# Attention scores over 64 rows in both row halves, from separate q and k

## The chip, the cores and the metric

The kernel runs on one core of one Trainium2 chip. The metric is the device time of one launch in microseconds. Before the change three runs took 1321.24 to 1322.76 us, with a median of 1322.1 us. The profile comes from one more execution.

## The reference

The kernel computes one transformer layer in fp32. There are 16 sequences of 256 tokens with 128 features.

```
x = x + attention(layernorm(x))        # 16 heads of 64
q, k, v = x @ Wq, x @ Wk, x @ Wv       # [16, 256, 16, 64]
w = softmax(q @ k.T / sqrt(64))
attention = (w @ v) @ Wo + bo
x = x + ffn(layernorm(x))              # 160 experts, top 8 of sigmoid scores
routed = sum over the chosen experts of weight * w_down @ silu(w_gate @ x)
shared = w_down_shared @ silu(w_gate_shared @ x)
```

## The kernel before, in words

The program has two stages. The first does attention, routing and the scatter of the normalised tokens into expert blocks of 64 rows in DRAM (`slot_x`). The second loads these blocks, runs the experts over them, stores the results (`block_y`), and gathers and combines them per token. The change touches the first stage alone.

The first stage is a software pipeline that is written out by hand and has the same form on each engine: `body(b)` for sequence b, with a loop over the 8 head pairs g. `step = 8 b + g`. In one body an engine works on several steps at once: on TensorE the scores of step - 1, the first products psY of this step, the values of every second step, the probabilities times values (psO) of step - 3, the transposes of the probabilities (psT) of step - 2, and the output projection (psA) of step - 4. Sequences 0 to 3 and the drain are straight code, 4 to 15 a hardware loop (`sequences`). All instructions of an engine run in the order of the code. Waits are on semaphores, which count how often a producer has finished: `p_ok` counts the exponentials (four a step), `s_ps` the scores of a head (two a step), `yq_ps`, `yh_ok` and `yl_ok` the psY products and their high and low parts, `c_in` and `x_in` the loads of small constants and of the tokens behind the first sequence.

Scores are not formed from q and k. At the start TensorE forms, for each head, m = Wq Wk^T (L529, 64 rows deep, heads alternating), and ScalarE and VectorE split m into a high and a low part (L645, L909). Then y = m^T x for two heads (psY), and the scores are y times the normalised tokens themselves, which ScalarE copies per sequence as `key_hi` and `key_lo` (L659, L660). Each product of split operands takes three matmuls: high by high, high by low, low by high (`split_product`). Matmuls of the scores run over all 128 rows of the array, first all six of head 0, then the six of head 1.

After the scores VectorE takes the negated row maxima (`negmax`, L1085), ScalarE the exponentials (L668), VectorE the reciprocal of the row sums (`rinv`), GpSimd three of the four multiplies by it (L795) and ScalarE the fourth (L682). TensorE transposes the result into psT, ScalarE copies it to `pT_sb` (L278).

From sequence 2 on VectorE also computes the routing of the sequence two before, one piece in each head pair (`choose`, `slots`, ... `blocks`), for which TensorE adds the ranks (L504 to L511, at g = 1), and GpSimd scatters 16 rows of indices by indirect DMA (L820), three or four of them in each of the head pairs 6, 7, 0, 1 and 2.

SyncE issues the loads in the order of the code, then the zero fill of `slot_x` and later parts of the fill and the expert weights, paced by `s_ps`.

Of the kernel before, what the change touches and what calls it, by code (L numbers as in the profile page):

```python
# [23 lines left out]
P = 128  # L24
# [39 lines left out]
def build(nc, x, wqT, wkT, wv, wo, bo, rwT, ebias, wgd, wgsT, wdsT, out):  # L64
# [4 lines left out]
    with ExitStack() as ctx:  # L69
# [36 lines left out]
        with actx:  # L106
# [61 lines left out]
            m_hi = sa("m_hi", [D, H, D], F32R)  # L168
            m_lo = sa("m_lo", [D, H, D], F32R)
# [7 lines left out]
            key_hi = sa("key_hi", [D, SEQ], F32R)  # L177
            key_lo = sa("key_lo", [D, SEQ], F32R)
            y_hi = sa("y_hi", [D, 2, 2, SEQ], F32R)
            y_lo = sa("y_lo", [D, 2, 2, SEQ], F32R)  # L180
# [13 lines left out]
            wqT_sb = sa("wqT_sb", [P, G, D])  # L194
            wkT_sb = sa("wkT_sb", [P, G, D])
# [31 lines left out]
        for name in """x0_in x_in wq_in wk_in wv_in c_in we_in zfill_a zfill_b yfill m_ps w_hi_ok w_lo_ok  # L227
                ln1_st ln1_ag ln1_ve ln1_rs ln1_xn xt_ps xt_hi xt_lo key_ok
# [55 lines left out]
        def _(sp):  # L284
            xv = x.rearrange("b s d -> (b s) d").rearrange("(n p) d -> p n d", p=P)
            sp.dma_start(x_res[:, 0:TB, :], xv[:, 0:TB, :]).then_inc(s["x0_in"], 16)
            sp.dma_start(wqT_sb[:], wqT.rearrange("(g p) d -> p g d", p=P)).then_inc(s["wq_in"], 16)
            sp.dma_start(wkT_sb[:], wkT.rearrange("(g p) d -> p g d", p=P)).then_inc(s["wk_in"], 16)
            sp.dma_start(wv_sb[:], wv).then_inc(s["wv_in"], 16)
            sp.dma_start(x_res[:, TB:NT, :], xv[:, TB:NT, :]).then_inc(s["x_in"], 16)  # L290
# [101 lines left out]
        def _(pe):  # L392
# [6 lines left out]

            def body(b):  # L400
                for g in range(G):
                    step = G * b + g
                    if live(b, g, 1):
                        u = step - 1
                        wait(pe, s["yh_ok"], u + 1)
                        wait(pe, s["yl_ok"], u + 1)
                        wait(pe, s["key_ok"], 2 * b if g == 0 else 2 * b + 2)
                        for h in range(2):
                            wait(pe, s["p_ok"], 4 * u - 2 + 2 * h)
                            for qt in range(TB):  # L410
# [228 lines left out]
        def _(act):  # L639
            act.wait_ge(s["wv_in"], 16)  # L640
            act.copy(wv_hi[:], wv_sb[:]).then_inc(s["w_hi_ok"], 1)
            act.wait_ge(s["m_ps"], 1)
            for k in range(4):

                act.activation(heads(m_hi, k), (psS, psT)[k // 2][:, k % 2, :].rearrange("p (g d) -> p g d", g=4),  # L645
                               ACT.Copy, scale=DH ** -0.5).then_inc(s["w_hi_ok"], 1)

            def body(b):
                for g in range(G):
                    step = G * b + g  # L650
                    if live(b, g, 0):
                        wait(act, s["yq_ps"], step + 1)
                        wait(act, s["s_ps"], 2 * (step - 1))
                        act.copy(y_hi[:, g % 2].rearrange("p a t -> p (a t)"), psY[:, 0, :]).then_inc(s["yh_ok"], 1)  # L654
                    if g == 0 and live(b, g, 0):
                        wait(act, s["s_ps"], 2 * step)
                        wait(act, s["xt_hi"], b + 1)
                        wait(act, s["xt_lo"], b + 1)
                        act.copy(key_hi[:], xnT_hi[:].bitcast(F32)).then_inc(s["key_ok"], 1)  # L659
                        act.copy(key_lo[:], xnT_lo[:].bitcast(F32)).then_inc(s["key_ok"], 1)  # L660
# [206 lines left out]
        def _(dve):  # L867
# [22 lines left out]
            def input_split(b):  # L890
# [14 lines left out]
            dve.wait_ge(s["w_hi_ok"], 1)  # L905
            dve.tensor_tensor(wv_lo[:], wv_sb[:], wv_hi[:].bitcast(F32), ALU.subtract).then_inc(s["w_lo_ok"], 1)
# [345 lines left out]
```

## Time and profile before

| | |
|---|---|
| median of three runs | 1322.1 us |
| the profiled execution | 1333.29 us, span 1331.9 us |
| mean granted TensorE clock | 0.835 |
| busy, TensorE, VectorE, ScalarE, GpSimd | 940.9, 848.5, 684.3, 740.5 us |
| attention with routing | from 22 us to about 735 us |
| q1, all loads and stores | 110.56 MB |

The profiled execution is 11.2 us above the median. Busy time of an engine is the time in which one of its instructions runs; TensorE's matmuls overlap, so its busy time is not its load. "Idle before" an instruction is followed by what released it. In the tables PE is TensorE, PEld its weight loads, DVE VectorE, ACT ScalarE, POOL GpSimd and SP SyncE.

### The profile page before, as it was taken

Reading aid. Unit: us, or ns where it says so; the run is one execution under the profiler, and the core shown is the slowest. Engines: PE = TensorE matmul, PEld = TensorE weight load, DVE = VectorE, ACT = ScalarE, POOL = GpSimd, SP = SyncE. Lnnn points to the kernel's source line nnn. Section 1 sums busy time; section 2 is a strip of 40 time slices with the busy share of each in tenths; the row PEclk is TensorE's granted clock in tenths of the full one; section 3 lists DMA queues with packets and bytes.
Section 4 is the critical chain, followed back from the end, with each engine's and each line's share of the span. In section 5 each row is a group of like instructions: output and inputs, shape, how many; then the busy total and the mean of one; then the engine's idle time right before and its main releaser. Section 6 shows DMA issues by size and latency. Waiting matters only on the chain.

```text
span 1331.9 us, 30438 instructions
## 1 busy us (share of the span) xinstructions
PE 940.9 (71%) x8654; PEld 770.8 (58%) x8654; DVE 848.5 (64%) x2817; ACT 684.3 (51%) x2015; POOL 740.5 (56%) x989
## 2 busy tenths in 40 slices
PE   4999999999999999999999448955566657200000
PEld 3888888878888888888887226633444445100000
DVE  3568889888888888888888635732555445532222
ACT  2878777777777777777778103722333333100000
POOL 1334766776676567666766570044443344677774
PEclk7999999999999999999999656966876677555555
DMA  8402432333233000012220624843544444221211
GB/s 298 190 1 96 155 120 114 120 121 117 112 122 120 18 20 32 24 51 77 91 81 22 259 85 133 266 129 130 156 158 155 141 137 143 87 59 58 57 57 35
DMA packets 64252, 144.65 MB, mean 109 GB/s; under 512 B 12496, under 2 KB 20624, under 8 KB 64208
## 3 DMA queue, kind: packets, MB, share of 16 engines
q1 hardware_dynamic: 47824, 110.56, 23.2%
q0 software_dynamic: 16384, 33.59, 8.3%
q8 instruction: 18, 0.29, 0.1%
q14 instruction: 26, 0.21, 0.1%
HBM read 59.16 MB, written 84.93 MB: 108 GB/s over the span
## 4 chain that ended last, share of the span: by engine, by line
PE 38%; issue 19%; DVE 14%; POOL 12%; ACT 6%; another core or an unknown queue 6%; DVEq 3%; DMA 1%; ACTq 0%; POOLq 0%; SPq 0%
POOL yg L843 10%; PE psS L396 8%; PE psT L449 6%; PE psY L396 5%; PE psO L434 5%; DVE w_b L1182 4%; ACT p_sb L668 3%; PE psS L606 2%; PE psA L459 2%; PE psT L596 2%; DVEq L245 2%; PE psVM L396 1%; POOL slot_x L820 1%; DVE xn L887 1%
## 5 line engine op out<-in xcount | busy, mean ns | idle before, releaser
L843 POOL DMA_INDIRECT yg<-block_y,tok_idx x256 | 247.3, 966 | 253.0 <-DMA block_y<-y_b 110.8
L795 POOL TENSOR_SCALAR p_sb<-p_sb,rinv 128x256 f32<-128x256 f32 x384 | 191.3, 512 | 219.5 <-DVE rinv L1075 215.0
L820 POOL DMA_INDIRECT slot_x<-xn_src,slot_u x256 | 255.7, 999 | 79.7 <-issue 75.4
L668 ACT ACTIVATE p_sb<-psS,negmax 128x256 f32<-128x256 f32 x512 | 236.6, 480 | 31.8 <-DVE negmax L1085 30.7
L1182 DVE COPY w_b<-w_all 128x192 f32 x672 | 129.9, 265 | 156.5 <-remote 106.3
L1085 DVE TENSOR_REDUCE negmax<-psS 128x2 f32<-128x512 f32 x256 | 167.4, 684 | 30.6 <-PE psS L396 14.4
L396 PE MATMUL psS<-key_hi,y_hi 128*128 128x256 f32 x512 | 157.8, 308 | 7.2 <-ACT p_sb L668 5.7
L434 PE MATMUL psO<-pT_sb,v_sb 128*64 128x256 f32 x1024 | 138.8, 391 | 21.6 <-ACT pT_sb L278 21.4
L278 ACT COPY pT_sb<-psT 128x512 f32<-128x512 f32 x256 | 141.7, 617 | 12.4 <-PE psT L449 6.6
L396 PE MATMUL psS<-key_hi,y_lo 128*128 128x256 f32 x512 | 144.7, 283 | 0.0
L396 PE MATMUL psS<-key_lo,y_hi 128*128 128x256 f32 x512 | 144.6, 282 | 0.0
L449 PE MATMUL psT<-ident,p_sb 128*128 128x128 f32 x1024 | 138.1, 278 | 2.1 <-POOL p_sb L795 2.1
L449 PEld LDWEIGHTS psT<-ident,p_sb 128*128 128x128 f32 x1024 | 113.5, 142 | 27.4 <-issue 18.8
L654 ACT CAST y_hi<-psY 128x512 fp32r<-128x512 f32 x128 | 75.1, 587 | 100.8 <-PE psY L396 96.6
L606 PE MATMUL psS<-xbT,w_b 128*64 128x64 f32 x1344 | 82.2, 256 | 60.6 <-issue 56.2
L1189 DVE TENSOR_TENSOR yg<-yg,wE_res 128x1024 f32<-128x1024 f32 x32 | 39.1, 1221 | 119.9 <-DMA yg<-block_y,tok_idx 119.5
L1090 DVE TENSOR_TENSOR y_lo<-psY,y_hi 128x512 fp32r<-128x512 f32 x128 | 87.7, 685 | 41.1 <-ACT y_hi L654 39.0
L606 PEld LDWEIGHTS psS<-xbT,w_b 128*64 128x64 f32 x1344 | 63.7, 162 | 86.0 <-issue 85.3
L668 ACT ACTIVATION_READ_ACCUMULATOR p_sb<-psS,negmax 128x1 f32 x512 | 108.0, 211 | 0.0
L396 PEld LDWEIGHTS psS<-key_hi,y_hi 128*128 128x128 f32 x512 | 97.7, 191 | 11.9 <-ACT p_sb L668 6.4
L396 PEld LDWEIGHTS psS<-key_lo,y_hi 128*128 128x128 f32 x512 | 97.9, 191 | 0.0
L396 PEld LDWEIGHTS psS<-key_hi,y_lo 128*128 128x128 f32 x512 | 97.4, 190 | 0.0
(175 smaller groups left out, 2107.8 us busy)
## 6 DMA issues: line engine op xcount, KB each, us to landing
block_y<-zero SPq DMA_DIRECT2D x21, 1024.0 KB
xb<-slot_x SPq DMA_DIRECT2D x84, 256.0 KB
block_y<-y_b SPq DMA_DIRECT2D x84, 256.0 KB
w_all<-in_wgd_dram SPq DMA_DIRECT2D x16, 960.0 KB
slot_x<-zero SPq DMA_DIRECT2D x1, 11264.0 KB, 34.3
slot_x<-zero SPq DMA_DIRECT2D x10, 1024.0 KB
slot_x<-xn_src,slot_u POOLq DMA_INDIRECT x256
yg<-block_y,tok_idx POOLq DMA_INDIRECT x256
```

Source lines behind the costliest of these rows:

```text
L278: copy(pT_sb[:, (g - 2) % 2, h].rearrange("p a t -> p (a t)"), psT[:, h, :]).then_inc(s[f"pt{h}_ok"], 1)
L396: m = pe.matmul(dst, wsl[a], xsl[c], start=(n == 0), stop=(n == 2))
L434: m = pe.matmul(psO[h * DH:(h + 1) * DH, 0, 0:SEQ], v_sb[:, (g - 3) // 2 % 2, kt, (g - 3) % 2, h * DH:(h + 1) * DH], pT_sb[:, (g - 3) % 2, ...
L449: m = pe.transpose(psT[:, h, kt * SEQ + qt * P:kt * SEQ + (qt + 1) * P], p_sb[:, (g - 2) % 2, h, qt, kt * P:(kt + 1) * P], ident[:])
L606: m = pe.matmul(psS[half, par, cols], w_b[:, r, i, 0:INTER], xbT[:, par, :, i * P // GB:(i + 1) * P // GB], start=True, stop=True)
L668: act.activation(p_sb[:, (g - 1) % 2, h, qt, :], psS[:, h, qt * SEQ:(qt + 1) * SEQ], ACT.Exp, bias=negmax[:, (g - 1) % 2, h, qt:qt + 1], s ...
L795: pool.tensor_scalar(pq, pq, rinv[:, (g - 1) % 2, k // 2, k % 2:k % 2 + 1], 1.0, ALU.mult, ALU.mult).then_inc(s["pn_ok"], 1)
L820: pool.indirect_dma_start(slot_x, bass.IndirectOffsetOnAxis(ap=slot_u[:, i, j:j + 1], axis=0), xn2_src[:, i, :], None).then_inc(s["scat"], 16)
L843: pool.indirect_dma_start(yg[:, r, k, :], None, block_y, bass.IndirectOffsetOnAxis(ap=tok_idx[:, par, r, k:k + 1], axis=0)).then_inc(gat[r ...
L1085: dve.tensor_reduce(negmax[:, (g - 1) % 2, h, :], psS[:, h, :].rearrange("p (i k) -> p i k", i=TB), AX.X, ALU.max, negate=True).then_inc(s ...
L1090: dve.tensor_tensor(y_lo[:, g % 2].rearrange("p a t -> p (a t)"), psY[:, 0, :], y_hi[:, g % 2].rearrange("p a t -> p (a t)").bitcast(F32), ...
L1182: m = dve.tensor_copy(w_b[:, r, i, :], w_all[:, bass.ds(e, 1), :].rearrange("p o i -> p (o i)"))
```

## The change

q and k are now formed as such. Wq and Wk are loaded as they are; ScalarE rounds them to their high parts (Wq with the factor 1/8) and VectorE forms the low parts, as both do for Wv. psY of a step holds q of the head pair in its first 256 columns and k in its second, with the two heads in the two halves of its partitions. Both are split into `qk_hi` and `qk_lo`. The score of a head then has 64 rows: head 0 in partitions 0 to 63, head 1 in 64 to 127. The new function `scores` alternates between the two heads at each matmul; each head has its own bank of psS. The three-way split stays.

With m go its 32 products and its split, with the keys go the two copies per sequence and `key_ok`. TensorE waits before all scores of a step for all four exponentials of the step before; it waited for two before head 0 and for four before head 1. Both heads raise `s_ps` at the end of the group.

Waits at the start move to the first use: `c_in` on TensorE from before the first product to the output projection of step 4, on VectorE to head pair 6 of sequence 1; `x_in` on VectorE to head pair 4 of sequence 0. The load of the remaining tokens is issued last of the first loads.

```diff
@@ SyncE
-            sp.dma_start(wqT_sb[:], wqT.rearrange("(g p) d -> p g d", p=P)).then_inc(s["wq_in"], 16)
-            sp.dma_start(wkT_sb[:], wkT.rearrange("(g p) d -> p g d", p=P)).then_inc(s["wk_in"], 16)
+            sp.dma_start(wq_sb[:], wq).then_inc(s["wq_in"], 16)
+            sp.dma_start(wk_sb[:], wk).then_inc(s["wk_in"], 16)
             sp.dma_start(wv_sb[:], wv).then_inc(s["wv_in"], 16)
-            sp.dma_start(x_res[:, TB:NT, :], xv[:, TB:NT, :]).then_inc(s["x_in"], 16)
...
             sp.dma_start(wds_sb[:], wdsT).then_inc(s["c_in"], 16)
+            sp.dma_start(x_res[:, TB:NT, :], xv[:, TB:NT, :]).then_inc(s["x_in"], 16)
@@ TensorE
+            def scores(par):
+                for qt in range(TB):
+                    q = (par, 0, slice(qt * P, (qt + 1) * P))
+                    for n, (a, c) in enumerate(((qk_hi, qk_hi), (qk_hi, qk_lo), (qk_lo, qk_hi))):
+                        for h in range(2):
+                            r = slice(h * DH, (h + 1) * DH)
+                            m = pe.matmul(psS[:, h, qt * SEQ:(qt + 1) * SEQ], a[(r, *q)], c[r, par, 1, :],
+                                          start=(n == 0), stop=(n == 2))
+                            if qt == TB - 1 and n == 2:
+                                m.then_inc(s["s_ps"], 1)
...
-                        wait(pe, s["key_ok"], 2 * b if g == 0 else 2 * b + 2)
-                        for h in range(2):
-                            wait(pe, s["p_ok"], 4 * u - 2 + 2 * h)
...
+                        wait(pe, s["p_ok"], 4 * u)
+                        scores((g - 1) % 2)
...
-                        for h in range(2):
-                            split_product(psY[:, 0, h * SEQ:(h + 1) * SEQ], (m_hi[:, 2 * g + h, :], m_lo[:, 2 * g + h, :]),
-                                          (xnT_hi[:], xnT_lo[:]), s["yq_ps"] if h == 1 else None)
+                        cols = slice(g * P, (g + 1) * P)
+                        for i, (hi, lo) in enumerate(((wq_hi, wq_lo), (wk_hi, wk_lo))):
+                            split_product(psY[:, 0, i * SEQ:(i + 1) * SEQ], (hi[:, cols], lo[:, cols]),
+                                          (xnT_hi[:], xnT_lo[:]), s["yq_ps"] if i == 1 else None)
...
+                        if isinstance(b, int) and step == 4:
+                            pe.wait_ge(s["c_in"], 16 * (4 + 2 * TB))
...
-            for g in range(G):
-                for h in range(2):
-                    r = slice(h * DH, (h + 1) * DH)
-                    m = pe.matmul((psS, psT)[g // 4][:, h, g % 4 * D:(g % 4 + 1) * D], wqT_sb[r, g, :], wkT_sb[r, g, :],
-                                  start=True, stop=True)
-            m.then_inc(s["m_ps"], 1)
-            pe.wait_ge(s["w_hi_ok"], 5)
-            pe.wait_ge(s["w_lo_ok"], 5)
-            pe.wait_ge(s["c_in"], 16 * (4 + 2 * TB))
+            pe.wait_ge(s["w_hi_ok"], 3)
+            pe.wait_ge(s["w_lo_ok"], 3)
@@ ScalarE
+            act.wait_ge(s["wq_in"], 16)
+            act.activation(wq_hi[:], wq_sb[:], ACT.Copy, scale=DH ** -0.5).then_inc(s["w_hi_ok"], 1)
+            act.wait_ge(s["wk_in"], 16)
+            act.copy(wk_hi[:], wk_sb[:]).then_inc(s["w_hi_ok"], 1)
...
-                        act.copy(key_hi[:], xnT_hi[:].bitcast(F32)).then_inc(s["key_ok"], 1)
-                        act.copy(key_lo[:], xnT_lo[:].bitcast(F32)).then_inc(s["key_ok"], 1)
@@ VectorE
+            dve.scalar_tensor_tensor(out=wq_lo[:], in0=wq_sb[:], scalar=DH ** -0.5, in1=wq_hi[:].bitcast(F32), op0=ALU.mult,
+                                     op1=ALU.subtract).then_inc(s["w_lo_ok"], 1)
+            dve.wait_ge(s["w_hi_ok"], 2)
+            dve.tensor_tensor(wk_lo[:], wk_sb[:], wk_hi[:].bitcast(F32), ALU.subtract).then_inc(s["w_lo_ok"], 1)
...
-            dve.wait_ge(s["x_in"], 16)
...
-            dve.wait_ge(s["c_in"], 16 * (4 + 2 * TB))
```

On TensorE, the scores of step 1 in the first sequence stand before the change like this. The names are the matmul's output and inputs; the brackets hold the semaphores that an instruction waits for.

```order
L396 MATMUL psS<-key_hi,y_hi 128x256 [waits key_ok,p_ok,yl_ok,yh_ok]
L396 MATMUL psS<-key_lo,y_hi 128x256
L396 MATMUL psS<-key_hi,y_lo 128x256
L396 MATMUL psS<-key_hi,y_hi 128x256
L396 MATMUL psS<-key_lo,y_hi 128x256
L396 MATMUL psS<-key_hi,y_lo 128x256
L396 MATMUL psS<-key_hi,y_hi 128x256 [waits p_ok]
```

And now the same scores on TensorE, with the psY product behind them:

```order
L406 MATMUL psS<-qk_hi 128x256 [waits p_ok,yl_ok,yh_ok]
L406 MATMUL psS<-qk_hi 128x256
L406 MATMUL psS<-qk_lo,qk_hi 128x256 x2
L406 MATMUL psS<-qk_hi,qk_lo 128x256 x2
L406 MATMUL psS<-qk_hi 128x256 x2
L406 MATMUL psS<-qk_lo,qk_hi 128x256 x2
L406 MATMUL psS<-qk_hi,qk_lo 128x256 x2
L395 MATMUL psY<-xnT_hi,wq_hi 128x256 [waits yl_ok]
```

The count of twelve is the same; the second wait for `p_ok` has gone into the first, and the heads alternate. At TensorE's start, before the change:

```order
L517 MATMUL psVM<-ident,xn 128x128 [waits ln1_xn,consts]
L517 MATMUL psVM<-ident,xn 128x128
L529 MATMUL psS<-wkT_sb,wqT_sb 128x128 [waits wk_in,wq_in]
L529 MATMUL psS<-wkT_sb,wqT_sb 128x128 x7
L529 MATMUL psT<-wkT_sb,wqT_sb 128x128 x8
L396 MATMUL psY<-xnT_hi,m_hi 128x256 [waits xt_hi,c_in,xt_lo,w_lo_ok,w_hi_ok]
```

And now at TensorE's start:

```order
L526 MATMUL psVM<-ident,xn 128x128 [waits ln1_xn,consts]
L526 MATMUL psVM<-ident,xn 128x128
L395 MATMUL psY<-xnT_hi,wq_hi 128x256 [waits xt_hi,xt_lo,w_lo_ok,w_hi_ok]
L395 MATMUL psY<-xnT_lo,wq_hi 128x256
L395 MATMUL psY<-xnT_hi,wq_lo 128x256
```

The products that form m are gone, and the first psY no longer waits for `c_in`.

## Rows read from the trace of the kernel before

**Rows 1.** Busy time by stretch: length, each engine, then granted clock, DMA share, GB/s.
```profile
22.00:24.00 2.00, 1.74 (x8) 1.77 (x9) 0.00 (x0) 0.08 (x1) 0.00 (x0) 0.50 1.02 422
...
62.00:103.00 41.00, 41.00 (x340) 35.68 (x336) 25.03 (x59) 33.49 (x105) 13.32 (x27) 1.00 0.01 1
...
549.00:594.00 45.00, 42.55 (x348) 36.66 (x346) 38.29 (x123) 33.80 (x104) 30.73 (x45) 1.00 0.13 45
```

**Rows 2.** Timeline of TensorE, one step: start, length, instruction, idle before.
```profile
546.29 0.36 PE L396 MATMUL psS<-key_hi,y_hi 128*128 128x256 f32 x1
...
547.80 0.28 PE L396 MATMUL psY<-xnT_hi,m_hi 128*128 128x256 f32 x1
...
548.61 1.08 PE L434 MATMUL psO<-pT_sb,v_sb 128*64 128x256 f32 x8
549.62 0.39 PE L396 MATMUL psVM<-wv_hi,xnT_hi 128*128 128x256 f32 x1
...
550.44 1.04 PE L449 MATMUL psT<-ident,p_sb 128*128 128x128 f32 x8
551.31 0.61 PE L459 MATMUL psA<-wo_sb,oT_sb 128*128 128x128 f32 x4
551.72 0.38 PE L396 MATMUL psS<-key_hi,y_hi 128*128 128x256 f32 x1
```

**Rows 3.** Timeline of GpSimd, multiplies of the first two steps.
```profile
31.54 1.41 POOL L795 TENSOR_SCALAR p_sb<-p_sb,rinv 128x256 f32<-128x256 f32 x3 [25.25 <-DVE rinv L1075]
...
35.74 0.48 POOL L795 TENSOR_SCALAR p_sb<-p_sb,rinv 128x256 f32<-128x256 f32 x1 [2.79 <-DVE rinv L1075]
```

**Rows 4.** Waits of one sequence, 549.5 to 594.3 us: total, times, longest.
```profile
POOL p_sb L795 <- DVE rinv L1075: 9.8, 5, 3.8
ACT y_hi L654 <- PE psY L396: 4.4, 3, 2.1
...
DVE rank_sb L943 <- PE psVM L511: 2.2, 1, 2.2
...
DVE y_lo L1090 <- ACT y_hi L654: 1.3, 2, 0.7
```

**Rows 5.** The chain that ended last, from 536 us: start, length, what.
```profile
541.68 1.43 PE psS L396 x12
...
549.50 0.70 DVE negmax L1085
...
552.16 1.34 another core or an unknown queue
```

**Rows 6.** Timeline of head pair 7 in a full sequence.
```profile
587.86 0.28 PE L396 MATMUL psY<-xnT_hi,m_hi 128*128 128x256 f32 x1
...
588.86 0.59 ACT L654 CAST y_hi<-psY 128x512 fp32r<-128x512 f32 x1 [1.75 <-PE psY L396]
...
591.06 0.22 ACT L668 ACTIVATION_READ_ACCUMULATOR p_sb<-psS,negmax 128x1 f32 x1
...
589.48 0.69 DVE L1090 TENSOR_TENSOR y_lo<-psY,y_hi 128x512 fp32r<-128x512 f32 x1 [0.72 <-ACT y_hi L654]
```

**Rows 7.** Timeline of the start, all engines.
```profile
6.19 0.66 PE L517 MATMUL psVM<-ident,xn 128*128 128x128 f32 x2 [6.19 <-DVE xn L887]
...
7.25 2.08 PE L529 MATMUL psS<-wkT_sb,wqT_sb 64*128 64x128 f32 x16 [0.39 <-DMA wkT_sb<-in_WkT_dram]
...
8.79 1.04 ACT L641 CAST wv_hi<-wv_sb 128x1024 fp32r<-128x1024 f32 x1 [6.77 <-DMA wv_sb<-in_Wv_dram]
...
9.87 1.22 DVE L906 TENSOR_TENSOR wv_lo<-wv_sb,wv_hi 128x1024 fp32r<-128x1024 f32 x1 [2.10 <-ACT wv_hi L641]
...
22.26 0.55 PE L396 MATMUL psY<-xnT_hi,m_hi 128*128 128x256 f32 x1 [11.43 <-issue]
...
22.40 0.33 PEld L396 LDWEIGHTS psY<-xnT_lo,m_hi 128*128 128x128 f32 x1
```

**Rows 8.** The instructions of L529: duration in ns, least, median, most.
```profile
L529 PEld LDWEIGHTS psS<-wkT_sb,wqT_sb x16: 285/330/335, 7.2 to 8.7; 64*128 64x128 f32 x16
```

More of the change, by code:

```diff
@@ L61, with build @@
 assert sum(SCAT) == TB * TOPK
-def build(nc, x, wqT, wkT, wv, wo, bo, rwT, ebias, wgd, wgsT, wdsT, out):
+def build(nc, x, wq, wk, wv, wo, bo, rwT, ebias, wgd, wgsT, wdsT, out):
     slot_x = nc.dram_tensor("slot_x", [NBLK * HB, D], F32).ap()
@@ L165, in build @@
             winv = sa("winv", [P, TB])
-            m_hi = sa("m_hi", [D, H, D], F32R)
-            m_lo = sa("m_lo", [D, H, D], F32R)
+            wq_hi = sa("wq_hi", [D, H * DH], F32R)
+            wq_lo = sa("wq_lo", [D, H * DH], F32R)
+            wk_hi = sa("wk_hi", [D, H * DH], F32R)
+            wk_lo = sa("wk_lo", [D, H * DH], F32R)
             wv_hi = sa("wv_hi", [D, H * DH], F32R)
@@ L176, in build @@
             xnT_lo = sa("xnT_lo", [D, SEQ], F32R)
[L177 to L180, printed above, removed]
+            qk_hi = sa("qk_hi", [P, 2, 2, SEQ], F32R)
+            qk_lo = sa("qk_lo", [P, 2, 2, SEQ], F32R)
             v_sb = sa("v_sb", [P, 2, TB, 2, P])
@@ L193, in build @@
             zero = sa("zero", [P, 8 * D])
-            wqT_sb = sa("wqT_sb", [P, G, D])
-            wkT_sb = sa("wkT_sb", [P, G, D])
+            wq_sb = sa("wq_sb", [D, H * DH])
+            wk_sb = sa("wk_sb", [D, H * DH])
             wv_sb = sa("wv_sb", [D, H * DH])
@@ L226, in build @@
         s = {}
-        for name in """x0_in x_in wq_in wk_in wv_in c_in we_in zfill_a zfill_b yfill m_ps w_hi_ok w_lo_ok
-                ln1_st ln1_ag ln1_ve ln1_rs ln1_xn xt_ps xt_hi xt_lo key_ok
+        for name in """x0_in x_in wq_in wk_in wv_in c_in we_in zfill_a zfill_b yfill w_hi_ok w_lo_ok
+                ln1_st ln1_ag ln1_ve ln1_rs ln1_xn xt_ps xt_hi xt_lo
                 yq_ps yh_ok yl_ok v_ps v_ok s_ps nm_ok p_ok ri_ok pn_ok pna_ok t_ps pt0_ok pt1_ok o_ps ot_ok ao_ps
@@ L653, in body @@
                         wait(act, s["s_ps"], 2 * (step - 1))
[L654 to L658, printed above, removed]
-                        act.copy(key_hi[:], xnT_hi[:].bitcast(F32)).then_inc(s["key_ok"], 1)
-                        act.copy(key_lo[:], xnT_lo[:].bitcast(F32)).then_inc(s["key_ok"], 1)
+                        act.copy(qk_hi[:, g % 2].rearrange("p a t -> p (a t)"), psY[:, 0, :]).then_inc(s["yh_ok"], 1)
                     if live(b, g, 1):
@@ L905, in _ @@
             dve.wait_ge(s["w_hi_ok"], 1)
-            dve.tensor_tensor(wv_lo[:], wv_sb[:], wv_hi[:].bitcast(F32), ALU.subtract).then_inc(s["w_lo_ok"], 1)
-            for k in range(4):
-                dve.wait_ge(s["w_hi_ok"], k + 2)
-                dve.scalar_tensor_tensor(out=heads(m_lo, k), in0=(psS, psT)[k // 2][:, k % 2, :].rearrange("p (g d) -> p g d", g=4),
-                                         scalar=DH ** -0.5, in1=heads(m_hi, k).bitcast(F32), op0=ALU.mult,
-                                         op1=ALU.subtract).then_inc(s["w_lo_ok"], 1)
-            dve.wait_ge(s["x_in"], 16)
+            dve.scalar_tensor_tensor(out=wq_lo[:], in0=wq_sb[:], scalar=DH ** -0.5, in1=wq_hi[:].bitcast(F32), op0=ALU.mult,
+                                     op1=ALU.subtract).then_inc(s["w_lo_ok"], 1)
+            dve.wait_ge(s["w_hi_ok"], 2)
+            dve.tensor_tensor(wk_lo[:], wk_sb[:], wk_hi[:].bitcast(F32), ALU.subtract).then_inc(s["w_lo_ok"], 1)
+            dve.wait_ge(s["w_hi_ok"], 3)
+            dve.tensor_tensor(wv_lo[:], wv_sb[:], wv_hi[:].bitcast(F32), ALU.subtract).then_inc(s["w_lo_ok"], 1)
             dve.wait_ge(consts, 5)
@@ L1089, in body @@
                         wait(dve, s["s_ps"], 2 * (step - 1))
-                        dve.tensor_tensor(y_lo[:, g % 2].rearrange("p a t -> p (a t)"), psY[:, 0, :],
-                                          y_hi[:, g % 2].rearrange("p a t -> p (a t)").bitcast(F32), ALU.subtract).then_inc(s["yl_ok"], 1)
+                        dve.tensor_tensor(qk_lo[:, g % 2].rearrange("p a t -> p (a t)"), psY[:, 0, :],
+                                          qk_hi[:, g % 2].rearrange("p a t -> p (a t)").bitcast(F32), ALU.subtract).then_inc(s["yl_ok"], 1)
                     if g == 7 and live(b, g, 0):
@@ L1125, in body @@
                         if g == 6:
+                            if isinstance(b, int) and b == 1:
+                                dve.wait_ge(s["c_in"], 16 * (4 + 2 * TB))
                             wait(dve, s["lg_ps"], b)
@@ L1130, in body @@
                     if g == 4 and live(b, g, 0):
+                        if isinstance(b, int) and b == 0:
+                            dve.wait_ge(s["x_in"], 16)
                         ln_stats(b + 1, "ln1", st1, mv1, ve1)
```

16 lines of the change are left out of this document (2 added, 14 removed).

## The prediction

> **What bounds the kernel now.** I read the busy time by stretch first, then one step and one sequence in the timeline, then the waits and the chain of that sequence. A share over the whole span would mix a start, two light sequences, fourteen full ones and the expert stage. By stretch there are two regimes: in the second sequence (62 to 103 us) TensorE is busy for 41.00 of 41 us and VectorE for 25.03; in a later one TensorE has 42.55 and VectorE 38.29 of 45 us [rows 1].
>
> In the first two sequences (16 steps) TensorE sets the pace, and a step is the sum of its work: scores 1.51 us for 12 matmuls, psY 0.81, psO 1.01, values 0.82, psT 0.87, psA 0.41, together 5.4 us, and 4.6 without values [rows 2]. That fits the 41 us of eight steps, 5.0 on average, with the extras. Only the very first three full steps, where psO, psT and psA are not all there yet, run at 4.20 us [rows 3].
>
> In the fourteen full sequences (some 44.9 us each) the waits show another bound. VectorE waits 2.2 us for the ranks and 1.3 us for ScalarE's y_hi, and little else; GpSimd waits 9.8 us in all, in the half without scatters; ScalarE waits 4.4 us for psY [rows 4]. The chain that ended last passes through the scores once per sequence, in head pair 7, and then through psY, y_hi, VectorE's y_lo and block table, the maxima, the exponentials, a hold of 1.34 us for which no releaser is known, v_sb, psT, psO, the ranks [rows 5]. So VectorE with GpSimd's scatters bounds these, and TensorE's scores count in one pair of eight: there y_lo waited 0.72 us for y_hi, which waited for psY [rows 6].
>
> At the start TensorE stands 11.43 us, up to 22.26 us, before its first product [rows 7].
>
> **The start.** That product waits for the rounded weights and for every small constant (c_in), and VectorE's first y_lo waits for c_in and the rest of x. The change moves these waits to step 4 and behind it; it also takes out 32 matmul records and the eight passes that split m. Added are two more roundings on ScalarE and two more low parts on VectorE. By the rows of wv, which has the same elements, these are 1.04 and 1.22 us each [rows 7]. wv landed at 8.79 us, with 2 MB of x issued behind it that now come last, and ScalarE can round wq and wk before that. VectorE had been free for 2.10 us at 9.87, so since 7.77: wq_lo until 9.0, wk_lo until 10.2, wv_lo until 11.5, and the first product at 11.6 instead of 22.26: **10.7 us less**. Bounds: wv_lo straight behind ScalarE gives 11.1 us; three weights landing 3 us later give 14.6. So 7.7 to 11.2 us. Late next are the constants at step 4 and x at VectorE's head pair 4. Both had landed by 22.26 in today's order, the same bytes in another order should have by then too, and these steps come at about 30 us, so I count them at nothing. If the zero fill, now issued behind x, held x back by 10 us more, that would cost 2 us.
>
> **The scores on TensorE.** Twelve matmuls over 128 rows become twelve over 64 rows, alternating between the row halves and between two banks. Do two halves run side by side? The kernel before shows it once, in the products L529: 64 rows, halves and banks alternating. Sixteen records take 2.08 us there, 0.13 each; two transposes of the same 128 columns over all 128 rows just ahead take 0.66 us, 0.33 each with the longer start of the first [rows 7]. Later, at the full clock, eight such records of psT take 0.87 us, 0.11 each [rows 2], which would be 0.22 at half the clock. L529's loads of 330 ns are as long as the one of 0.33 us at 22.40, where the granted clock was 0.50 (1.2 GHz) [rows 1, 7, 8], so both are at the lower level. Halves side by side: a factor of about 2.
>
> At that rate 12 matmuls of 0.12 us need 0.72 us instead of 1.44. A change of shape is not free: psY takes 0.81 up to the start of psO and the values 0.82 behind it, where six times 0.12 is 0.72 [rows 2], so 0.1 us each way, and the first score today has 0.07 of its own. I take 1.0 us for the group: **0.5 us less** on TensorE in every step. Bounds: 0.72 (side by side, free switches) and 1.85 (one after another, and 0.2 us at either end).
>
> The Trainium skill, TensorEngine Tiling (Array Packing), Key Properties, says that changing the tiling mode drains TensorE; the 0.1 us at psO agree with it. TensorE: Matmul & The Clock Gate, Part 3 of the Trainium skill, gives 3.07x for four row tiles. An estimate by that page, three quarters of the ideal, would make the group 0.96 us and the switches, 1.2 in all.
>
> **What that is worth.** The scores now wait for all four exponentials of the step before (p_ok 4u), where head 0 went ahead after two. Queued behind the waiting score on TensorE are psY, psO and psT, and ScalarE and VectorE wait for psY, so a loop closes: 0.1 us for the semaphore, scores 1.0, psY to y_hi 1.00 (587.86 to 588.86), y_hi and four exponentials 2.42 (to 591.06 + 0.22) [rows 6]: 4.5 us. Steps of 4.6 become 4.5, those of 5.4 become 4.9, the three of 4.20 grow to 4.5. Thirteen steps by -0.32, three by +0.3: **3 us less**; bounds, with a group of 0.72 or 1.85, -7 and +10.
>
> In the fourteen full sequences head pair 7 gets its psY 0.5 us earlier, and y_lo follows, out of its 0.72: 14 x 0.5 = **7 us less**; bounds -10 and +5. In the other pairs TensorE idles or VectorE comes to the maxima after the scores are done: VectorE is the late one. The two key copies on ScalarE go (0.7 us a sequence). They lie between y_hi and the exponentials of head pair 0, which in the chain were released by negmax at 549.50 + 0.70 [rows 5]; I count them at nothing, and nothing is late behind them.
>
> Sum against the profiled execution's own 1333.29 us: -10.7 - 3 - 7 = -20.7, so 1312.6. That execution lies 11.2 us above the median of 1322.1, which gives **1301.4**, 1.6% less. Its own range by the bounds around it is 1292 to 1310.
>
> **Rivals.**
> 1. Only the start pays. For it: GpSimd's scatters fill half of a sequence, and what head pair 7 wins can end in a wait for its multiply behind them. Against it: the chain went through ScalarE and VectorE there, not through GpSimd [rows 5]. 1322.1 - 10.7 = 1311.4.
> 2. The hold moves. ScalarE stands 1.34 us shortly after each turn of the loop [rows 5], and its loop body loses two copies with their waits. Twelve turns without it give 16 to 17 us more, 1285; twice as long, 1318. For it: the hold has no releaser in the profile; against: it is there in the same place in sequence after sequence. The Trainium skill, Runtime: NRT & Kernel Launch, Instruction fetch mechanics, says that a taken branch out of the fetched window stalls for the fetch. By that the hold stays, tied to the branch; no row here shows a fetch.
> 3. Slower: the halves do not run side by side with fp32r weights, and the group takes 1.85 us. The place is the loop above, then 5.35 us: three steps +1.15 and thirteen about +0.5, +10 in all; full sequences 0.34 x 14 = +5; less 10.7 at the start: +4.3, 1326.4. It decides from a group of about 1.75 us on, where the loss reaches the gain of the start. Against it: the 0.13 us of L529, though these are fp32 weights with 128 columns.
>
> **Numbers.** Forecast 0.58, only the start 0.21, hold gone 0.10, hold doubled 0.04, halves not side by side 0.07. The range from 1284 to 1318 leaves out the slow case and the tails. About 0.2% (2.6 us) is what a measurement of this kernel can tell from no change. Faster by more: the forecast, the start alone and most of the hold's cases, 0.90. Within it 0.04, slower 0.06.
>
> **What would show it.** The first psY at 11.6 us, and no wait for x or constants behind it. Twelve scores in 1.0 us up to the first psY. GpSimd's multiplies 4.5 and 4.9 us apart in the second sequence. A full sequence of 44.4 us, and y_lo's wait of 0.72 down to 0.2. I am wrong if scores start 0.12 us apart (rival 3), if a full sequence keeps 44.9 (rival 1), or if the hold is gone or doubled (rival 2); and most of all if sequences shrink by several us, since then VectorE and GpSimd were not the bound.

## The result and the profile after

The changed kernel took a median of 1310.05 us (four runs, 1307.38 to 1311.6), the kernel before 1322.43 us beside it: a ratio of 0.9902, with a 95% interval of 0.9879 to 0.9925, or 12.3 us less. Timed once more, beside the experiments, it took 1173.97 us against 1202.56 us: a ratio of 0.9769 (0.9747 to 0.9792), 28.6 us less. Both kernels are faster there, and the change is worth more. The forecast of 20.7 us less lies between. I call these the first and the second measurement; all experiments belong to the second, which ran on three chips that agree (1200.9 to 1202.6 us for the kernel before). The first profile of the changed kernel has an own time of 1309.07 us and a span of 1307.8 us, 1.0 us below its median, so the 11.2 us by which the profiled execution before lay above its median did not carry over.

The start, in the timeline of the first profile of the changed kernel (start, length, instruction, idle time before it with its releaser):

```profile
5.09 1.06 ACT L641 ACTIVATE wq_hi<-wq_sb 128x1024 fp32r<-128x1024 f32 x1 [3.06 <-DMA wq_sb<-in_Wq_dram]
...
9.98 1.22 DVE L903 TENSOR_TENSOR wv_lo<-wv_sb,wv_hi 128x1024 fp32r<-128x1024 f32 x1
11.30 0.55 PE L395 MATMUL psY<-xnT_hi,wq_hi 128*128 128x256 f32 x1 [4.43 <-DVE wv_lo L903]
...
19.11 0.58 PE L406 MATMUL psS<-qk_hi 64*128 64x256 f32 x2 [2.60 <-ACT p_sb L661]
19.46 0.45 PE L406 MATMUL psS<-qk_lo,qk_hi 64*128 64x256 f32 x2
```

The first psY starts at 11.30 us, released by the last low part and by no load; it was 22.26 us [rows 7]. The second group of scores stood 2.60 us for the exponentials and then ran at 0.21 us a pair of matmuls. Why, the busy time by stretch shows (length, each engine's busy time, granted clock, DMA share, GB/s):

```profile
17.00:19.00 2.00, 0.00 (x0) 0.00 (x0) 0.70 (x2) 1.96 (x9) 0.00 (x0) 0.81 1.04 294
19.00:22.00 3.00, 2.90 (x18) 2.70 (x19) 1.41 (x3) 0.51 (x1) 1.41 (x3) 0.50 1.00 330
22.00:25.00 3.00, 3.00 (x16) 2.92 (x15) 0.92 (x3) 2.63 (x10) 0.00 (x0) 0.50 1.03 418
25.00:28.00 3.00, 3.00 (x28) 2.03 (x26) 1.57 (x3) 2.55 (x7) 2.09 (x4) 0.99 1.03 421
...
62.00:103.00 41.00, 40.48 (x358) 32.75 (x356) 29.54 (x76) 33.53 (x105) 14.14 (x27) 1.00 0.07 27
...
549.00:594.00 45.00, 40.48 (x356) 32.02 (x352) 38.51 (x125) 33.88 (x104) 31.10 (x45) 1.00 0.20 67
```

TensorE did nothing from 17 to 19 us, and from 19 to 25 us it has the lower of its two clocks, 1.2 GHz. Below, TensorE's share in a full sequence fell from 42.55 to 40.48 of 45 us, while VectorE's rose from 38.29 to 38.51 and GpSimd's from 30.73 to 31.10 [rows 1].

One step on TensorE, in the timeline of the changed kernel:

```profile
553.12 0.38 PE L406 MATMUL psS<-qk_hi 64*128 64x256 f32 x2
553.35 0.28 PE L406 MATMUL psS<-qk_lo,qk_hi 64*128 64x256 f32 x2
553.46 0.28 PE L406 MATMUL psS<-qk_hi,qk_lo 64*128 64x256 f32 x2
553.58 0.28 PE L406 MATMUL psS<-qk_hi 64*128 64x256 f32 x2
553.70 0.28 PE L406 MATMUL psS<-qk_lo,qk_hi 64*128 64x256 f32 x2
553.82 0.28 PE L406 MATMUL psS<-qk_hi,qk_lo 64*128 64x256 f32 x2
554.02 0.39 PE L395 MATMUL psY<-xnT_hi,wq_hi 128*128 128x256 f32 x1
```

Each row is two matmuls, one per head, and rows follow 0.12 us apart, as single matmuls over 128 rows did. The group takes 0.90 us up to psY, in the median of all steps 0.91, against 1.51 before [rows 2]: the halves run side by side, 6 x 0.12 = 0.71, and 0.2 us of the group goes on the changes of shape. These cost more outside the group. From psA to psO in one step of the second sequence, in the kernel before:

```profile
74.30 0.61 PE L459 MATMUL psA<-wo_sb,oT_sb 128*128 128x128 f32 x4
74.67 0.36 PE L396 MATMUL psS<-key_hi,y_hi 128*128 128x256 f32 x1
...
76.17 0.28 PE L396 MATMUL psY<-xnT_hi,m_hi 128*128 128x256 f32 x1
...
76.98 1.08 PE L434 MATMUL psO<-pT_sb,v_sb 128*64 128x256 f32 x8
```

and in the changed kernel:

```profile
72.38 0.61 PE L468 MATMUL psA<-wo_sb,oT_sb 128*128 128x128 f32 x4
72.92 0.39 PE L406 MATMUL psS<-qk_hi 64*128 64x256 f32 x2
...
73.83 0.39 PE L395 MATMUL psY<-xnT_hi,wq_hi 128*128 128x256 f32 x1
...
74.73 1.08 PE L441 MATMUL psO<-pT_sb,v_sb 128*64 128x256 f32 x8
```

From psA to the first score it is now 0.54 us instead of 0.37, and from psY to psO 0.90 instead of 0.81. The whole stretch falls from 2.68 to 2.35 us: TensorE saves 0.33 us, not the 0.6 us by which the group is shorter, and steps with values went from 5.39 to 5.06 us. The Trainium skill, TensorEngine Tiling (Array Packing), Key Properties, says that a change of tiling mode drains TensorE; the longer passages on either side agree.

The multiplies of head pairs 7 and 0 on GpSimd, in the same profile:

```profile
569.72 1.39 POOL L788 TENSOR_SCALAR p_sb<-p_sb,rinv 128x256 f32<-128x256 f32 x3 [3.76 <-DVE rinv L1065]
571.29 1.10 POOL L813 DMA_INDIRECT slot_x<-xn_src,slot_u  x1 [0.17 <-issue]
...
574.95 1.40 POOL L788 TENSOR_SCALAR p_sb<-p_sb,rinv 128x256 f32<-128x256 f32 x3
...
581.39 1.62 POOL L788 TENSOR_SCALAR p_sb<-p_sb,rinv 128x256 f32<-128x256 f32 x3
```

And VectorE in head pair 7:

```profile
572.49 0.69 DVE L1080 TENSOR_TENSOR qk_lo<-psY,qk_hi 128x512 fp32r<-128x512 f32 x1 [0.32 <-ACT qk_hi L653]
```

The low part now waits 0.32 us instead of 0.72 [rows 6]. But the multiply at 574.95 has no idle time ahead of it: three scatters and a multiply fill the 5.23 us of this head pair. It had been 5.46 us, with 0.26 us idle. A full sequence came from some 44.9 us to 44.6 or 44.7.

By the copies of the ranks, once in a sequence, the changed kernel's lead in the first two profiles is 13.6 us at sequence 2, 16.5 at 3, 17.1 at 9, 18.6 at the second last, and 14.7 at the last. The rest of the 24.1 us between the two spans, 9.4 us, is in the expert stage, where the change does nothing. That is most of the 11.2 us by which the execution before lay above its median.

### The profile page after: what moved, and what is told of

Its sections match the earlier page's. It is cut to its first block, busy times and chain, and to the rows that moved or that the text cites. A ratio compares the mean times of both kernels' runs of the same rounds, so it can differ in the third digit from the quotient of the medians.

```text
span 1307.8 us, 30227 instructions
## 1 busy us (share of the span) xinstructions
PE 905.3 (69%) x8622; PEld 692.6 (53%) x8622; DVE 849.2 (65%) x2815; ACT 672.3 (51%) x1981; POOL 739.6 (57%) x989
## 4 chain that ended last, share of the span: by engine, by line
PE 34%; issue 22%; DVE 17%; POOL 14%; ACT 6%; DMA 3%; another core or an unknown queue 2%; DVEq 2%; POOLq 0%; SPq 0%; ACTq 0%
POOL yg L836 10%; PE psS L606 5%; PE psS L406 4%; PE psY L395 4%; ACT p_sb L661 4%; PE psO L441 4%; PE psT L596 3%; PE psT L456 3%; DVE negmax L1075 3%; POOL slot_x L813 3%; PE psO L617 2%; PE psY L617 2%; DVE qk_lo L1080 2%; DVE le L1018 1%
## 5 line engine op out<-in xcount | busy, mean ns | idle before, releaser
L441 PE MATMUL psO<-pT_sb,v_sb 128*64 128x256 f32 x1024 | 142.3, 399 | 18.1 <-ACT pT_sb L278 13.3
L606 PE MATMUL psS<-xbT,w_b 128*64 128x64 f32 x1344 | 86.5, 258 | 61.1 <-issue 57.4
L653 ACT CAST qk_hi<-psY 128x512 fp32r<-128x512 f32 x128 | 74.8, 584 | 87.5 <-PE psY L395 81.8
L406 PE MATMUL psS<-qk_hi 64*128 64x256 f32 x512 | 86.2, 331 | 42.4 <-ACT p_sb L661 38.1
L1080 DVE TENSOR_TENSOR qk_lo<-psY,qk_hi 128x512 fp32r<-128x512 f32 x128 | 87.4, 683 | 15.9 <-ACT qk_hi L653 15.3
L441 PEld LDWEIGHTS psO<-pT_sb,v_sb 128*64 128x64 f32 x1024 | 64.6, 138 | 55.6 <-issue 14.9
L713 ACT ACTIVATE h_b<-psS 128x256 f32<-128x256 f32 x84 | 33.0, 393 | 97.6 <-remote 86.5
L406 PEld LDWEIGHTS psS<-qk_hi 64*128 64x128 f32 x512 | 49.2, 186 | 64.0 <-ACT p_sb L661 43.1
L596 PE MATMUL psT<-ident,xb 128*128 128x128 f32 x336 | 69.5, 333 | 18.8 <-issue 13.8
L468 PE MATMUL psA<-wo_sb,oT_sb 128*128 128x128 f32 x512 | 78.3, 275 | 1.5 <-DVE oT_sb L1088 1.5
```

The source lines that it names most:

```text
L406: m = pe.matmul(psS[:, h, qt * SEQ:(qt + 1) * SEQ], a[(r, *q)], c[r, par, 1, :], start=(n == 0), stop=(n == 2))
L441: m = pe.matmul(psO[h * DH:(h + 1) * DH, 0, 0:SEQ], v_sb[:, (g - 3) // 2 % 2, kt, (g - 3) % 2, h * DH:(h + 1) * DH], pT_sb[:, (g - 3) % 2, ...
L606: m = pe.matmul(psS[half, par, cols], w_b[:, r, i, 0:INTER], xbT[:, par, :, i * P // GB:(i + 1) * P // GB], start=True, stop=True)
L1080: dve.tensor_tensor(qk_lo[:, g % 2].rearrange("p a t -> p (a t)"), psY[:, 0, :], qk_hi[:, g % 2].rearrange("p a t -> p (a t)").bitcast(F32 ...
```

## The experiments

**Only the start as before.**

```diff
+            pe.wait_ge(s["c_in"], 16 * (4 + 2 * TB))      # before the first product
+            dve.wait_ge(s["x_in"], 16)                    # and the same on VectorE, with c_in
-            sp.dma_start(x_res[:, TB:NT, :], ...)         # last
+            sp.dma_start(x_res[:, TB:NT, :], ...)         # ahead of wo_sb
```

> The changed kernel, but with the load of the remaining tokens in its old place ahead of the small constants, and TensorE and VectorE waiting for all of them before the first product, as before the change. The scores part alone is left. Theory (the start pays nearly all): the first psY comes at 22 us again, and the time is 11 us above the changed kernel, 1320 to 1322 us. Rival (the scores pay as forecast, 10 us of the 20.7): the first psY at 22 us, but the lead in the sequences stays, so the time is below 1315 us. Second rival (the old order of loads is not what holds the first psY, the split of m was): the first psY at 12 to 15 us and the time within 3 us of the changed kernel.

1185.58 us, ratio 0.9868 (0.9843 to 0.9894), 11.6 us above the changed kernel as timed later. TensorE's timeline:

```profile
21.50 0.55 PE L395 MATMUL psY<-xnT_hi,wq_hi 128*128 128x256 f32 x1 [14.61 <-DMA wds_sb<-in_wdsT_dram]
```

The last small constant held the first psY. The 11 us of the start hold. But 16 us of gain are left without it, so "the start pays nearly all" fell: here the scores pay more than forecast.

**Only the waits moved, in the kernel before.**

```diff
-            pe.wait_ge(s["c_in"], 16 * (4 + 2 * TB))      # before the first product
+                        if isinstance(b, int) and step == 4:
+                            pe.wait_ge(s["c_in"], 16 * (4 + 2 * TB))
...
```

> The kernel before with only the waits at the start moved: c_in on TensorE to step 4 and on VectorE to head pair 6 of sequence 1, x_in to head pair 4 of sequence 0, and the load of the remaining tokens issued last. m, its split, the scores over 128 rows and the key copies stay. In the first trace VectorE had finished the last m_lo at 13.99 us. Theory (the waits are the start's gain, and a start that is earlier comes off the end one to one): the first psY at 14.1 instead of 22.3 us, 8 us less time. Rival (the gain of the start is lost later, at the zero fill and the scatters that it delays): 3 us or less. Second rival (the loads of x, now last, come too late for head pair 4): first psY at 14.1 us, but a gap of 2 us or more on VectorE behind it.

1191.92 us, ratio 0.9923 (0.9906 to 0.9939), 9.0 us less. TensorE's timeline:

```profile
14.29 0.35 PE L396 MATMUL psY<-xnT_hi,m_hi 128*128 128x256 f32 x1 [3.25 <-issue]
```

The first psY came 7.3 us before that of the kernel before beside it (21.62), and all of it reached the end. No wait for x or constants is on record behind it. The two parts give 0.9923 x 0.9868 = 0.9792, at the upper edge of the interval of both together (0.9747 to 0.9792). Some 2.8 us are missing from a full sum. The two parts do not quite cover the change: with m still formed, the first psY comes at 14.29 us and not at 11.3, and these 3.0 us are in neither.

**One head after the other.**

```diff
-                    for n, (a, c) in enumerate(...):
-                        for h in range(2):
+                for h in range(2):
+                    wait(pe, s["p_ok"], 4 * u - 2 + 2 * h)
+                    for qt in range(TB):
+                        for n, (a, c) in enumerate(...):
```

> The changed kernel, but the six matmuls of head 0 run before the six of head 1, with a wait for two exponentials before head 0 and for four before head 1, as before the change. The start is that of the changed kernel. Theory (TensorE counts in the first two sequences only): without alternation the row halves do not run side by side, the group from its first matmul to the first psY is 1.4 to 1.5 us instead of 0.91, the first two sequences lose 2 to 4 us, full sequences under 0.3 us each; the time is 2 to 6 us above the changed kernel. Rival (full sequences need the fast scores): 0.5 us or more per full sequence, 10 us or more above. Second rival (only the start pays): within 2 us of the changed kernel.

1194.49 us, ratio 0.9935 (0.9916 to 0.9955): 20.5 us above the changed kernel. The theory is refuted and the first rival held: full sequences need the fast scores, by 1.2 to 1.3 us each (43.07 against 41.80 late in the stage). The group took 1.25 us, not 1.5. Its timeline, with psY behind it (x1 is one matmul, x2 one of each head):

```profile
645.28 0.38 PE L407 MATMUL psS<-qk_hi 64*128 64x256 f32 x1
645.50 0.28 PE L407 MATMUL psS<-qk_lo,qk_hi 64*128 64x256 f32 x1
645.62 0.28 PE L407 MATMUL psS<-qk_hi,qk_lo 64*128 64x256 f32 x1
645.63 0.39 PE L407 MATMUL psS<-qk_hi 64*128 64x256 f32 x2
645.85 0.28 PE L407 MATMUL psS<-qk_lo,qk_hi 64*128 64x256 f32 x2
645.97 0.28 PE L407 MATMUL psS<-qk_hi,qk_lo 64*128 64x256 f32 x2
646.09 0.28 PE L407 MATMUL psS<-qk_hi 64*128 64x256 f32 x1
646.21 0.28 PE L407 MATMUL psS<-qk_lo,qk_hi 64*128 64x256 f32 x1
646.33 0.28 PE L407 MATMUL psS<-qk_hi,qk_lo 64*128 64x256 f32 x1
646.53 0.39 PE L395 MATMUL psY<-xnT_hi,wq_hi 128*128 128x256 f32 x1
```

Head 1's first matmul starts 0.01 us behind head 0's third, although it stands behind head 0's sixth in the code: three matmuls of each head overlap (in 104 of the 128 steps here, in all 128 of the next experiment), so the order in the code did not keep the halves apart, and no run shows the halves fully one after another. The group is still 0.26 us shorter than before the change, but the step is not: in the second sequence steps take 5.41 and 4.65 us, against 5.39 and 4.63 before. The longer passages at the changes of shape (0.17 and 0.10 us) use it up.

**The same, with one wait for all four exponentials.**

```diff
+                        wait(pe, s["p_ok"], 4 * u)
-                    wait(pe, s["p_ok"], 4 * u - 2 + 2 * h)
```

> As the kernel that does one head after the other, but with one wait for all four exponentials ahead of both heads, as the changed kernel has it. The group stays at 1.25 us. Theory (the wait for four closes a loop of psS, psY, high part and exponentials): steps of the first two sequences of 4.8 to 4.85 and 5.4 us where the two-wait kernel has 4.65 and 5.40, so 1 to 2 us in them, and 0 to 5 us in full sequences: 1 to 7 us slower than the two-wait kernel. Rival (the wait costs nothing since the values fill it): within 1 us of it.

1193.6 us, ratio 0.9939 (0.9921 to 0.9957): no difference to two waits. In the second sequence steps without values went from 4.65 to 4.80 us and those with them stayed at 5.40, as the loop says, but in the late full sequences nothing is lost (42.87 and 43.08 us). The wait costs 0.15 us in each step without values of the second sequence, and in the time as a whole nothing that shows.

**Each score product twice.**

```diff
-                for qt in range(TB):
+                for qt, again in ((qt, again) for qt in range(TB) for again in range(2)):
```

> The changed kernel with each of the twelve score products done twice, halves still alternating, so 24 matmuls and 1.6 us instead of 0.91 up to the first psY. Theory (TensorE sets the pace of the first two sequences and has slack in most full ones): 16 x 0.7 = 11 us in the first two sequences' steps, 1 to 2 us per full sequence, so 20 to 40 us above the changed kernel, and slower than one head after the other by more than the 0.1 us in which the groups differ. Rival (TensorE has slack nearly everywhere): under 12 us above. Second rival (TensorE sets the pace in every step): 128 x 0.7 = 90 us above.

1219.48 us, ratio 1.0142 (1.0119 to 1.0165), 45.5 us above the changed kernel. The group takes 1.62 us, 0.72 more. The second sequence grew from 38.78 to 44.52 us, 0.72 for each of its eight steps; a late full one from 41.79 to 45.10, 3.3 us for eight times 0.72. So TensorE sets the pace of every step of the second sequence. In a late full one, at this length, six of the eight intervals between GpSimd's multiplies grew, by 0.15 to 1.34 us, and two did not. The forecast price of a longer group (0.34 us in one pair of eight) was far too low.

**The key copies back on ScalarE.**

```diff
+                        act.copy(key_hi[:], xnT_hi[:].bitcast(F32)).then_inc(s["key_ok"], 1)
+                        act.copy(key_lo[:], xnT_lo[:].bitcast(F32)).then_inc(s["key_ok"], 1)
```

> The changed kernel with the two copies of the normalised tokens per sequence back on ScalarE, in their old place between the high part of head pair 0 and its exponentials; nothing reads them. Theory (they lie where ScalarE waits for the maxima): within 1.5 us of the changed kernel. Rival (each copy delays the exponentials of head pair 0 by its 0.35 us): 16 x 0.7 = 11 us more.

1175.09 us, ratio 0.9773 (0.9751 to 0.9795), 1.1 us above the changed kernel: nothing that can be told from zero, as forecast.

**The kernel before once more, and the changed one.**

> The kernel before, unchanged, for a trace beside the other runs of this call. In the first trace of it step 1 of a full sequence took 7.2 us and ScalarE or VectorE stood some 1.3 to 1.8 us once per sequence with no releaser on record; in the four experiments so far no such hold is on record and that step takes 5.4 to 5.5. Theory (the hold belongs to the chip or the execution, not to the kernel): where the other kernels of this call show no hold, this one shows none, and a full sequence takes 43.0 to 43.8 us instead of 44.9. Rival (the hold belongs to this loop body and its place in memory): 44.9 us again.

> The changed kernel, unchanged, timed beside experiments. Theory (without the hold TensorE counts in more head pairs, so the scores pay more): the ratio to the kernel before is 0.975 to 0.982 (21 to 30 us), the first psY still at 11.3 us, and a full sequence 41.5 to 42 us in the trace where the zero fill is over. Rival (the same 12 us as in the first measurement): 0.988 to 0.992.

The ratio of the changed kernel is 0.9769 (0.9747 to 0.9792). In both traces the hold is gone. The waits of the first profile of the changed kernel from 195 to 690 us had (total, times, longest):

```profile
ACT pT_sb L278 <- remote: 17.3, 16, 1.8
DVE negmax L1075 <- remote: 11.0, 10, 1.2
ACT qk_hi L653 <- remote: 5.4, 2, 3.2
```

"remote" is a wait without a releaser on record. The first profile before has the same, 31.3 us in all. None of the twelve profiles of the second measurement has any in that stretch, and head pair 1 takes 5.4 us there instead of 7.0 to 7.2. It is the same program in both, so the hold belongs to the chip or the execution. Without it a late full sequence takes 42.87 us before and 41.79 after the change. Where the 1.08 us come from, GpSimd's multiplies show, first in the kernel before:

```profile
624.88 1.39 POOL L795 TENSOR_SCALAR p_sb<-p_sb,rinv 128x256 f32<-128x256 f32 x3 [0.44 <-DVE rinv L1075]
...
636.75 1.39 POOL L795 TENSOR_SCALAR p_sb<-p_sb,rinv 128x256 f32<-128x256 f32 x3
642.76 1.66 POOL L795 TENSOR_SCALAR p_sb<-p_sb,rinv 128x256 f32<-128x256 f32 x3 [0.86 <-DVE rinv L1075]
```

and in the changed kernel:

```profile
612.52 1.58 POOL L788 TENSOR_SCALAR p_sb<-p_sb,rinv 128x256 f32<-128x256 f32 x3
618.01 1.55 POOL L788 TENSOR_SCALAR p_sb<-p_sb,rinv 128x256 f32<-128x256 f32 x3
...
642.48 1.39 POOL L788 TENSOR_SCALAR p_sb<-p_sb,rinv 128x256 f32<-128x256 f32 x3
```

Head pair 2 (636.75 to 642.76, and 612.52 to 618.01) falls from 6.01 to 5.49 us, head pair 7 from 5.61 to 5.21: in both GpSimd had waited, and now its scatters and multiplies run without a gap. With the hold ScalarE was late in head pair 1 already, and the multiply of pair 2 came straight behind the scatters in both kernels, 5.80 us; so nothing was won there in the first measurement.

Between 223 and 444 us a sequence takes 43.3 to 45.4 us in this trace of the changed kernel. GpSimd's timeline there has such a row in four of the five sequences:

```profile
282.74 0.41 POOL L775 TENSOR_SCALAR xn_src<-xn 128x256 f32<-128x256 f32 x1 [1.64 <-DMA slot_x<-xn_src,slot_u]
```

It waits for the last scatter to land, while 1 MB zero fills of `block_y` go out. The kernel before has the same wait there, 1.9 us long, and takes 44.5 us a sequence. So the lead hardly grows in this stretch: it is 17.1 us at its start and 19.0 at its end, 0.4 us more a sequence.

**The scatters spread over six head pairs**, in the changed kernel and in the one before.

```diff
-SCAT = [3, 4, 3, 3, 3]
-SCAT_G = 6
+SCAT = [2, 3, 3, 3, 3, 2]
+SCAT_G = 5
```

> The changed kernel with the 16 scatters of a sequence spread over six head pairs, 2, 3, 3, 3, 3 and 2 from pair 5 on, instead of 3, 4, 3, 3 and 3 from pair 6 on. Theory (GpSimd takes over the pace in the changed kernel: its multiplies of pairs 7, 0, 2 and 3 follow the last scatter without a gap): the interval of 6.44 us behind four scatters falls to about 5.3, the 6.06 us of pair 3 by about 1, a full sequence from 44.6 to 42.5 to 43.5 us, and the time by 12 to 28 us to 1282 to 1298. Rival (VectorE sets the pace and GpSimd only fills it): a full sequence stays at 44.3 us or more, the time within 4 us of the changed kernel.

> The kernel before with the same spreading of the scatters, 2, 3, 3, 3, 3 and 2 from pair 5 on. Theory (GpSimd hid what the scores gained in full sequences): this kernel gains less from the spreading than the changed one, which then is 15 to 20 us faster than this one, not 12. Rival (the two edits do not touch each other): the distance stays at 12 us, within 2.

The changed kernel with it took 1148.07 us, ratio 0.9555 (0.9534 to 0.9577), 25.9 us below the changed kernel alone, within the 12 to 28 us of its theory; the kernel before with it 1176.36 us, 0.9784 (0.9757 to 0.9811), 26 us below itself. The sequences from 223 to 444 us fell to 41.3 us, as the late ones (the last of the five to 42.5), and the wait for the last scatter from five times, 7.6 us, to once, 1.4 us; the drain from the second last ranks to the last took 19.7 us instead of 25.5. The distance between the two stayed at 28.3 us, so in the time the two edits did not touch each other. The theory that the kernel before would gain less was wrong; the 12 us named in it came from the first measurement. Inside the sequences they do touch: by stretch, from 510 to 600 us, TensorE is now never idle in the kernel before,

```profile
510.00:600.00 90.00, 90.00 (x742) 78.63 (x740) 81.98 (x271) 73.36 (x226) 64.23 (x93) 1.00 0.17 58
```

and in the changed one it is:

```profile
510.00:600.00 90.00, 85.51 (x744) 68.04 (x745) 82.57 (x263) 72.90 (x221) 67.89 (x98) 1.00 0.22 72
```

A late full sequence takes 41.86 and 41.3 us, 0.55 apart instead of 1.08; the drain makes up for it (24.96 and 19.67 us).

**One copy in three head pairs from VectorE to ScalarE**, on top of the spread scatters, and with these at 3, 3, 3, 2, 3, 2.

```diff
+                    if live(b, g, 3) and g in (1, 3, 5):
...
+                        act.copy(oT_sb[:, (g - 3) % 2, :], psO[:, 0, 0:SEQ]).then_inc(s["ot_ok"], 1)
```

> The changed kernel with the scatters spread over six head pairs and, in head pairs 1, 3 and 5, the copy of psO to oT_sb on ScalarE instead of VectorE. Theory (with the scatters spread, VectorE sets the pace, at 41.3 us a full sequence, and has a queue behind each copy of 0.33 us): 0.5 to 1.0 us less per full sequence, 7 to 14 us less in all than with the scatters spread alone. Rival (ScalarE, 0.4 us later with its exponentials, gives it back): within 2 us. Second rival: slower by 2 us or more, as TensorE's psA and psO wait for ScalarE's queue.

> As the kernel just named, with the scatters at 3, 3, 3, 2, 3 and 2 from head pair 5 on, so that one fewer stands behind the multiplies of head pair 0 and one more behind those of pair 5. Theory (GpSimd had stood without a gap before the multiplies of pairs 7 and 1, and has 2.5 us free at pair 6): the interval of pair 1 loses 0.1 to 0.2 us, 1 to 3 us less in all. Rival (VectorE alone sets the pace): within 1 us.

1149.17 us, ratio 0.958 (0.9556 to 0.9604), and 1148.4 us, 0.9557 (0.9536 to 0.9578): no gain over the spread scatters alone. Head pair 5 became 0.22 us shorter and pair 3 0.2 us longer; a full sequence stays at 41.3. What bounds it at 41.3 was not settled. The spread scatters alone are the version that beats both kernels, by 4.5% and, against the changed kernel's 1173.97 us, by 2.2%.

## Why the prediction was right in sign and off in size

1. **The start, -10.7 us.** Right: 10.96 in the first profile and 10.3 in the second pair, psY at 11.3 where 11.6 was forecast, and one to one at the end (11.6 us by the old waits). Moved waits alone give 7 to 9 of it. x and the constants were not late.
2. **The group at 1.0 us, 0.5 us less in every step.** The group is right, 0.91, and rival 3 is out. The 0.5 us are not: the forecast put both changes of shape into its 1.0 us, and with the passages on either side they come to 0.91 + 0.17 + 0.10 = 1.18 us. Where TensorE sets the pace a step with values won 0.33 us.
3. **The first two sequences, -3 us.** The loop of 4.5 us was right (4.49 us in the second sequence). Steps with values took 5.06 us where 4.9 was forecast, by the same passages. The lead grew by 2.6 us up to the ranks of sequence 2, 1.7 in the second measurement. Missed was the first step at 5.81 us, where TensorE stood 2.60 us and then ran six microseconds at 1.2 GHz. That is a matter of the execution: with the scatters spread TensorE stood the same 2.60 us at the same place, its clock stayed at 1.00, and the step took 4.47 us.
4. **The full sequences, 14 x -0.5.** This is the step that failed, in size and both ways. In the first measurement a steady full sequence won 0.2 to 0.3 us, and the lead grew by 5.0 us from sequence 2 to the second last: y_lo's wait fell by 0.40, but the multiply of head pair 7 came to stand behind GpSimd's scatters, as rival 1 had it. In the second it won 1.08, in head pairs 2 and 7. "In the other pairs TensorE idles or VectorE comes to the maxima after the scores are done" was wrong without the hold: head pair 2 fell by 0.5 us with the shorter group, and a group longer by 0.72 us cost 3.3 us a sequence, not 0.7.
5. **The carry over of 11.2 us.** Wrong as a rule: 9.4 us of the spans' distance sat in the expert stage of the one execution. The drain, not in the sum, gave back 3.9 us of the lead in the first two profiles and none in the second pair; which scatter waits for which transfer there was not followed.
6. **The hold, rival 2.** It neither went nor doubled with the change (31.3 and 33.7 us in the first profiles) and is absent in both kernels in the second measurement. The Trainium skill, Runtime: NRT & Kernel Launch, Instruction fetch mechanics, ties such a stall to a taken branch out of the fetched window. The same program took the same branches without a hold, so that rule alone does not explain it; what does stays open, and no row shows a fetch.
7. **The range.** The forecast's own range of 1292 to 1310 us is not the sum of its bounds, which give 1294 to 1329.

So 12.3 us is start plus little. In the first two profiles the lead at the last ranks is 11.0 + 2.6 + 5.0 - 3.9 = 14.7 us, and the 2.4 us between that and the medians have no place. The 28.6 us are start plus some one microsecond in each full sequence: in the second pair of traces the lead grows from 12.0 to 25.5 us in thirteen sequences, steadily in the late ones (1.0 to 1.2 us each) and unevenly before (-0.8 to 2.1). That the missing hold makes the difference between the two is argued from the step times; no run switched it alone.

## What to carry to other kernels

Take a price per step from a table of intervals for every step of a period, with the idle time before the engine that ends it, not from the one step where the chain passes: a second engine with no gap (here GpSimd at 5.2 us behind three scatters) caps the gain, and a stall that may not be there next time hides another one. Move waits to their first use first; that came off the end one to one. Where one engine issues fixed blocks of work (16 scatters), try spreading them over more steps: six instead of five took 26 us off both kernels. And price a change of matmul shape by the whole stretch between two matmuls that did not change, not by the changed group alone: here 0.27 of the 0.60 us went there.

## What the runs showed of the hardware

- Two heads of 64 rows, alternating between row halves, ran at one pair in 0.12 us, the rate of one matmul over 128 rows. With one head after the other in the code, head 1's first three still ran beside head 0's last three (1.25 us for twelve, against 0.91).
- With 64 row matmuls between matmuls over 128 rows, psA to the first score took at least 0.54 us instead of 0.37, and psY to psO 0.91 instead of 0.81 in the median.
- TensorE's granted clock was 0.50 (1.2 GHz) from 19 to 25 us, after 2.60 us in which it did nothing between two groups. With the scatters spread it was 1.00 throughout, after the same 2.60 us. In the kernel before with moved waits and longer groups TensorE stood 1.69 us there and the first three steps took 4.20 us each, against 5.81, 4.74 and 4.48.
- The column of the granted clock can miss such a stretch: with the key copies pairs of score matmuls followed 0.21 us apart from 20.5 to 21.35 us, and the column reads 1.00 there. It reads 1.00 at L529 too; that these products ran at the lower level, as the forecast says, shows in the length of their weight loads, 0.33 us, where those of psA take 0.19 us at the full clock.
- The kernel before took 1322 us in the first measurement and 1201 to 1203 on the three chips of the second, with 571 and 450 us from the last ranks to the end in its two profiles.
